# Seven PSUM banks in the first layer's loop, its sums and a residue on GpSimd, half the maxima rows on ScalarE

## What is computed

```python
def _L0_conv_ref(x, w_proj, b_proj, w_out, b_out):
    tokens = x.reshape(B, C, N).transpose(0, 2, 1)
    qkv = (tokens @ w_proj + b_proj).reshape(B, N, NUM_HEADS, 3 * HEAD_DIM)
    q, k, v = jnp.split(qkv, 3, axis=-1)
    attn = jnp.einsum('bihd,bjhd->bijh', q, k) * SCALE
    attn = jax.nn.softmax(attn, axis=2)
    res = jnp.einsum('bijh,bjhd->bihd', attn, v).reshape(B, N, NUM_HEADS * HEAD_DIM)
    out = res @ w_out + b_out + tokens
    return out.transpose(0, 2, 1).reshape(B, C, H, W)
```

## Time and profile before

| | us |
|---|---|
| median of three runs | 3099.82 (3094.11 to 3104.37) |
| the profiled execution | 3101.73, span 3100.0 |
| TensorE busy in it | 2708.6 (87%), mean granted clock 0.935 |
| VectorE busy | 2196.4 (71%) |
| ScalarE busy | 1220.1 (39%) |
| GpSimd busy | 603.8 (19%) |

### The profile page before, as it was taken

One profiled execution on the slowest core, in us unless ns is written; L12 is line 12 of the kernel. 1 busy time (PEld: TensorE's weight loads), 2 busy tenths in 40 slices (PEclk: granted clock), 3 DMA queues, 4 the chain that ended last, 5 costly groups with the idle time before them and its releaser, 6 DMA issues.

```text
span 3100.0 us, 42243 instructions
## 1 busy us (share of the span) xinstructions
PE 2708.6 (87%) x14966; PEld 1854.5 (60%) x14966; DVE 2196.4 (71%) x2490; ACT 1220.1 (39%) x1348; POOL 603.8 (19%) x381
## 2 busy tenths in 40 slices
PE   5989979899898898988889888898888899888993
PEld 4447754577545775467754677447764477644772
DVE  4876678766687676867678576785678766787666
ACT  2443325433254333543335333353334533245334
POOL 0520116002160022500224002330024200242011
PEclk8999989999799998999989999899999999899996
DMA  6100050000500005000040001400022000310016
GB/s 154 27 25 1 1 130 1 25 1 14 117 1 25 1 14 117 1 25 1 21 110 1 25 1 38 93 7 19 1 69 62 25 1 1 94 37 25 1 55 244
DMA packets 46388, 124.57 MB, mean 40 GB/s; under 512 B 9792, under 2 KB 21312, under 8 KB 42560
## 3 DMA queue, kind: packets, MB, share of 16 engines
q1 hardware_dynamic: 46144, 121.41, 14.4%
HBM read 43.01 MB, written 23.86 MB: 22 GB/s over the span
## 4 chain that ended last, share of the span: by engine, by line
PE 69%; DVE 10%; ACT 8%; issue 6%; SPq 4%; DMA 3%; DVEq 0%; ACTq 0%
PE tile L1270 23%; PE pv L1270 10%; PE pv L1374 7%; PE tile L1364 6%; PE tile L1342 5%; ACT p L666 4%; PE tile L1515 4%; SPq L452 3%; PE tile L1394 3%; DMA stack<-qk_r 2%; DVE small L877 2%; PE tile L1537 2%; PE tile L1645 2%; PE tile L1564 1%; PE tile L1416 1%
## 5 line engine op out<-in xcount | busy, mean ns | idle before, releaser
L877 DVE TENSOR_REDUCE small<-tile 128x1 f32<-128x1024 f32 x512 | 612.6, 1220 | 125.0 <-PE tile L1342 121.1
L666 ACT ACTIVATE p<-tile 128x1024 f32<-128x1024 f32 x512 | 506.7, 1026 | 457.9 <-PE tile L1364 393.4
L1342 PE MATMUL tile<-stack 96*128 96x512 f32 x1024 | 356.9, 441 | 63.6 <-DMA stack<-qk_r 30.3
L1364 PE MATMUL tile<-stack 112*128 112x512 f32 x1024 | 369.0, 452 | 20.8 <-DVE small L877 14.1
L1270 PE MATMUL tile<-qk_r 128*128 128x512 f32 x1536 | 377.9, 395 | 0.0
L578 POOL TENSOR_TENSOR row_sum<-act 128x256 f32<-128x256 f32 x32 | 42.1, 1335 | 1640.0 <-DVE act L1105 1640.0
L553 POOL TENSOR_TENSOR acc<-acc,p 128x1024 f32<-128x1024 f32 x144 | 344.8, 2416 | 31.2 <-DVE acc L909 29.3
L1270 PEld LDWEIGHTS tile<-qk_r 128*128 128x128 f32 x1536 | 287.1, 188 | 66.4 <-issue 7.7
L1110 DVE TENSOR_TENSOR pl<-p,ph 128x1024 fp32r<-128x1024 f32 x128 | 158.2, 1236 | 238.0 <-ACT p L751 238.0
L1364 PEld LDWEIGHTS tile<-stack 112*128 112x128 f32 x1024 | 175.2, 196 | 241.7 <-issue 85.0
L1342 PEld LDWEIGHTS tile<-stack 96*128 96x128 f32 x1024 | 185.9, 202 | 187.2 <-ACT p L666 110.8
(11 more groups left out here) (277 smaller groups left out, 4256.0 us busy)
## 6 DMA issues: line engine op xcount, KB each, us to landing
stack<-qk_r SPq DMA_DIRECT2D x192, 256.0 KB, 5.0
x_in<-in_x_dram SPq DMA_DIRECT2D x9, 1024.0 KB, 7.6
act<-in_x_dram SPq DMA_DIRECT2D x8, 1024.0 KB, 8.0
x_scratch<-act SPq DMA_DIRECT2D x7, 1024.0 KB, 4.0
z_scratch<-zbuf SPq DMA_DIRECT2D x7, 1024.0 KB, 5.1
stack<-ones SPq DMA_DIRECT2D x8, 512.0 KB, 7.6
w3f<-w3f_scratch SPq DMA_DIRECT2D x8, 512.0 KB, 3.2
fin_rest<-z_scratch SPq DMA_DIRECT2D x3, 1024.0 KB, 12.7
```

What stands on the lines that cost most here:

```text
L666: sc.activation(p0[:, jt % DEPTH, pair, :], tile_wait(b, "st0", *u, jt, pair), ACT.Exp, scale=float(D) ** -0.5).then_inc(scalar_done, scal ...
L877: ve.tensor_reduce(maxima[:, h * NT + it:h * NT + it + 1], t[:], X, ALU.max).then_inc(vector_done, vector.one("max0", g, h, it))
L1342: ins = mm(o[:, s], stack[0:IMAX, 0, g, h, it * P:(it + 1) * P], stack[0:IMAX, 1, g, h, s], start=True, stop=True)
L1364: ins = mm(o[:, halves[k]], stack[0:K0, 1, g, h, jt * P:(jt + 1) * P], stack[0:K0, 0, g, h, halves[half]], start=True, stop=True)
```

## The change

1. In units 0 to 2 the six banks and the idle bank of `pv` are handed out in two rings. `s0`, `m0`, `den0` and (in units 1 and 2) `ex0` share two tiles of two banks. The scores have three single banks, one of them the idle half of `pv`, and one head to a bank: four `st0` and four `exp0` of 128x512 a step in place of two of 128x1024. The order in a step becomes `s0`, `st0`, `st0`, `s0`, `st0`, `st0`, `pv0`. Unit 3 keeps two heads to a tile and the three large tiles.
2. All ten `add0` of units 0 to 2 go to GpSimd.
3. `res_lo` of units 0 to 2 goes to GpSimd, behind the two additions of step 1 of the next unit. The bias `bv0` is no longer added in `res_hi` and `res_lo`: it is multiplied by the output weights once, in the setup, and comes in with the output bias.
4. Of the four `max_rows` of a unit VectorE keeps two. For the other two heads ScalarE runs four `max_cols`, each an activation of 16x2x128 out of `m0`'s tile with `mask8` as its scale, before the first `exp0` of the unit.

```diff
-POOL_BOTH = (1, 2, 4)
+POOL_BOTH = (1, 2, 3, 4, 5)
+    if next_unit(g, half):
+        return ("s0", 0), ("st0", 0), ("st0", 1), ("s0", 1), ("st0", 2), ("st0", 3)
+    return ("st0", 0), ("st0", 1)
...
+        s += [("pv0_out", *last_unit(*u))] if last_unit(*u) else []
+        s += [("max_cols", *u, t) for t in range(HT)]
...
-            s += [("res_lo", *last)] if last and jt == 3 else []
-            s += [("max_rows", *following, h) for h in range(G)]
+            s += [("max_rows", *following, h) for h in range(G // 2)]
...
+            s += [("add0", *u, jt, pair) for pair in range(2) if adder(*u, jt, pair) == "pool"]
+            s += [("res_lo", *last_unit(*u))] if last_unit(*u) and jt == 1 else []
...
+        ring = ("scores" if kind == "st0" else "rows") if looped else "whole"
+        if ring == "scores":
+            home[n] = ((2, 0), (2, 1), (3, 1 - n[2]))[rings[ring] % 3]
+        else:
+            home[n] = (rings[ring] % (2 if ring == "rows" else SLOTS), None)
...
+                            pool.wait_ge(scalar_done, scalar.at(b, "res_hi", g, half))
+                            pe.tensor_tensor(side[:, 1, g, cols_], raw[:, cols_], side[:, 0, g, cols_].bitcast(F32),
+                                             ALU.subtract).then_inc(pool_done, gps.one("res_lo", g, half))
...
+                    for t in range(HT):
+                        it = HT * half + t
+                        sc.activation(stack[IMAX:K0, 0, g, G // 2:G, it * P:(it + 1) * P], m, ID, scale=mask8[:, it:it + 1]
+                                      ).then_inc(scalar_done, scalar.one("max_cols", g, half, t))
```

More of the change, by code:

```diff
@@ L68, in last_unit, with score_tiles, heads_of, exp_of @@
     return UNITS[k - 1] if k else None
+def score_tiles(g, half):
+    return 2 if (g, half) == UNITS[-1] else G
+def heads_of(g, half, k):
+    n = G // score_tiles(g, half)
+    return range(n * k, n * k + n)
+def exp_of(g, half, jt, pair):
+    return ("exp0", g, half, jt, score_tiles(g, half) // 2 * (pair + 1) - 1)
+def key_tile(g, half):
+    if next_unit(g, half):
+        return ("s0", 0), ("st0", 0), ("st0", 1), ("s0", 1), ("st0", 2), ("st0", 3)
+    return ("st0", 0), ("st0", 1)
 def rows_of(unit, k):
@@ L244, in conv_seq_kernel, with banks, leavers @@
     place = {n: k for k, n in enumerate(tiles)}
-    def slot(*name):
[L247 to L255, removed]
+    home, rings = {}, {"whole": 0, "rows": 0, "scores": 0}
+    for n in tiles:
+        kind, unit, looped = n[0], n[1:3], False
+        if kind in ("st0", "den0"):
+            looped = unit != UNITS[-1]
+        elif kind == "s0":
+            looped = n[3] // HT + n[1] > 0
+        elif kind == "m0":
+            looped = unit != UNITS[0]
+        elif kind == "ex0":
+            looped = next_unit(*unit) not in (None, UNITS[-1])
+        ring = ("scores" if kind == "st0" else "rows") if looped else "whole"
[3 more added lines that the diff above has]
+            home[n] = (rings[ring] % (2 if ring == "rows" else SLOTS), None)
+        rings[ring] += 1
+    def slot(*name):
+        assert home[name][1] is None
+        return home[name][0]
+    def banks(name):
+        k, half = home[name]
+        return [(k, q) for q in range(2) if half in (None, q)]
+    def leavers(b, *name):
+        k, found = place[name], {}
+        for bank in banks(name):
+            users = [n for n in tiles[k + 1:] + tiles[:k] if bank in banks(n)]
+            if bank[0] == SLOTS:
+                users = [n for n in tiles[:k] if bank in banks(n) and n[1:3] == name[1:3]]
+            for engine, *step in last_readers(users[-1]) if users else ():
+                steps = {"scalar": scalar, "vector": vector}[engine]
+                now = place[users[-1]] < k
+                found[engine] = max(found.get(engine, (False, 0, None)), (now, steps.place[tuple(step)], tuple(step)))
+        return [(engine, ({"scalar": scalar, "vector": vector}[engine].at if now
+                          else {"scalar": scalar, "vector": vector}[engine].before)(b, *step))
+                for engine, (now, _, step) in found.items()]
     x_v = x.rearrange("b (t p) h w -> b p t (h w)", p=P)
@@ L595, in tile_wait @@
                 act_e.wait_ge(tensor_done, tensor.at(b, *name))
[L596 removed]
+                return where(*name)
             act_e.wait_ge(weights_in[0], 16)
@@ L686, in _ @@
                     last = last_unit(*u)
+                    if last:
+                        pv0_out(*last)
+                    max_cols(*u)
                     for jt in range(NT):
[L688 to L691, removed]
+                        for k in range(score_tiles(*u)):
+                            exp0(u, jt, k)
                         if last and jt == 2:
@@ L991, in _ @@
                                 add0(u, jt - 1, pair)
-                        if last and jt == 3:
-                            res_lo(*last)
                     if following:
```

120 lines of the change are left out of this document (74 added, 46 removed).

## The result

| | before | after |
|---|---|---|
| median us | 3102.1 (3094.11 to 3104.51, 4 runs) | 3209.07 (3203.78 to 3213.39, 4 runs) |
| the profiled execution | 3101.73, span 3100.0 | 3213.39, span 3211.7 |
| mean granted clock in it | 0.935 | 0.917 |

The account below looks back on a forecast made before the run. It took the tile ring to pace the old step and GpSimd's additions to hold `den0` after the change. Losses of 2.6 + 0.95 + 0.95 + 1.1 us a pass, 45 in all, plus 36 for the clock: median 3181; range 3115 to 3230.

Parts of the forecast that it names:

- GpSimd as the bound of units 1 and 2: Units 1 and 2: `den0` waits for GpSimd's additions and starts at 31.3 us instead of 30.35, plus 0.95 each.
- The step: Clean step of units 0 to 2: 3.2 us in place of 3.50 with three single banks for the scores.
- Unit 0: Start of unit 0: four `max_cols` delay the first `s0`, and `den0` starts at 491.3 instead of 488.67, plus 2.6 us.
- Unit 3: Start of unit 3: first scores fall into `den0`'s tile and wait for `rec0`, plus 1.1 us.
- The negation: End of a unit: three small VectorE operations negating the maxima; by the port rule up to two additions late.
- Rival 3: Negation blocked as well: 0.6 us more in each of 24 units and longer standstills, 3225 us; chance 8%.
- The clock: TensorE's clock falls to 0.50 around `den0` after standstills: 1.5 us for each of 24 stretches, 36 us.
- The sum at full clock: All units, clock held: 5.6 us a pass, 45 for eight passes, giving 3147 us on the profiled execution.
- VectorE gives up two `max_rows`: nothing: VectorE in each unit: two `max_rows` fewer, 1.24 us, gain nothing because `den0` covers them.
- Rival 2: TensorE sets the end: units 1 and 2 gain 2.4 us each, 3070 us in all; chance 6%.
- Rival 4: No change: `res_hi` earlier, `res_lo` and `max_cols` at low bounds, clock held, about 3108 us; chance 6%.
- rival 1: TensorE's clock holds through the waits before `den0`, all else as forecast, 3145 us; chance 25%.

Follow-up runs that it names:

- the five-step kernel: Changed kernel with GpSimd summing steps 1 to 4, `den0` taking step 5, all `max_rows` on VectorE, unit 3's first scores skipping `den0`'s tile: 3037.74 us, ratio 0.9798.
- The ring alone: Changed kernel with eight sums on GpSimd, `res_lo` on VectorE and no `max_cols`, keeping part 1 and the bias move: 3120.0 us, ratio 1.0071.
- the run with additions that need each other: Changed kernel with `res_lo` back on VectorE in step 3 and GpSimd adding pairs in order 0, 1, 1, 0, 0, 1: 3167.43 us, ratio 1.0223.
- the run with the order alone: Changed kernel, otherwise whole, with GpSimd's ten sums in pair order 0, 1, 1, 0, 0, 1: 3205.87 us, ratio 1.0359.

## Why the prediction held, and where it was short

The direction and the mechanism were right, and the time fell inside the range, 28 us above the forecast. By its own steps:

- **GpSimd as the bound of units 1 and 2: right.** Forecast were its start 5.2 into the unit, a pause of 1.0 before `res_lo`, and its end at 31.2. The rows have 5.2, 0.98 and 30.8. The residue took 1.28, near the 1.2 taken.
- **The step: nearly right.** 3.2 forecast, 3.08 measured; TensorE was through with `pv0` at 26.8, so the standstill before `m0` was 4.42, not 3.4.
- **Unit 0: right in kind, 2.6 forecast, 3.1 measured.** Four `max_cols` took 1.53 (1.9 taken). The run without the columns confirms that they are the cause. There `den0` comes 3.7 earlier than with them, so they cost more than the 3.1 that the change shows, and the rest of the change gains 0.6 in unit 0.
- **Unit 3: right.** 1.1 forecast, 1.0 in six passes, with the idle time before the first scores put down to `rec0`, as forecast. In two passes it was 2.2 and 2.5; these are the two in which the low clock lasted longest in unit 2's `den0` (5.3).
- **The negation: a case that was held for a rival.** The forecast put `den0` 0.1 behind GpSimd's last addition, with `m0` done before. Rival 3 said that the negation would be blocked and `m0` follow it. So it came (5.04 for `neg_hi`), and `den0` starts 1.40 after the last addition (543.23 to 544.63), of which 0.95 is `m0` at the low clock. This is why units 1 and 2 lost 1.84 and 1.74 and not 0.95 although GpSimd was 0.4 early. The rival had 8%, with the text's own reason for it, that the operations meet an addition every time. The chance was too low: nothing in the rows of before spoke for the negation getting in. The rival's reason, turns of one instruction each, is not what came either: `neg_hi` alone waited past two boundaries between additions.
- **The clock: the term that was mis-sized.** 36 us were taken, 1.5 for each `den0`, as the middle between 0 and 2.8. The run with TensorE kept busy measures 62 in all, 2.6 for each. In units 1 and 2 the low stretch covers most of `den0` (4.56 to 5.31 in place of 2.83, so 1.7 to 2.5 over); in unit 0 five of eight had none and three had 1.3 to 2.2. The `den0` stretches together are 39, near the 36, but `m0` and the stretches outside the loop had no term in the sum.
- **The sum at full clock: close by luck.** With the clock held the kernel has 3147 us, and the sum was 3145 on the median. The units of that run are 6.7 a pass longer than before, 53 in all, where 45 was forecast. Its time agrees because it is 8 shorter outside the loop, for which the forecast had no term.
- **"VectorE gives up two `max_rows`: nothing": right.** With them back, units 1 and 2 kept their 32.2. **The setup, under 1 us: not shown.** 2.4 us were lost before the first `m0`, where the setup lies, and no run splits them. The same stretch differs by up to 3.2 between runs with one and the same setup.

Rival 2, in which TensorE sets the end, is what the five-step kernel shows: with GpSimd done in time, all `max_rows` on VectorE and the tile skipped, the same ring gives 2.0%. The ring alone lost as well (25 us), since VectorE's operations then waited for GpSimd and unit 3's first scores for `rec0`. So most of the loss is in what went with the ring: GpSimd's longer queue, the standstills with the low clock behind them, and the columns in unit 0. Rival 4 did not come, and rival 1, the clock holding, came only in five of unit 0's eight waits.

## What to carry to other kernels

Give an engine with a small busy share its work by the deadline in the stage where it works: here GpSimd was at 19%, and ten additions in a unit made it the last to finish, where eight did not. Summing five steps, with all `max_rows` on VectorE and unit 3's tile skipped, turned 3.5% slower into 2.0% faster. When an edit makes a busy engine wait, count the low clock behind that wait near the upper bound and add what runs beside it: 2.6 us for each wait here, where 1.5 was taken. When VectorE works on SBUF beside GpSimd, look for the longest run of independent instructions on GpSimd, since that run, not one instruction, is what VectorE may have to wait for.

## What was not expected of the hardware

**VectorE can wait for several of GpSimd's instructions, not for one.** Beside GpSimd's additions of 2.38 us, an operation of VectorE whose tensors all lie in SBUF took up to 11.1 us (`res_lo`, 0.68 alone), 3.4 (128x1024 additions, 1.2 alone) and 5.07 (a 128x16 operation with one tensor as input, 0.17 alone). In each of these it ended 0.03 to 1.1 us after the end of an addition behind which GpSimd paused, if only for the 0.08 us in which the next addition waits for that one's result. The form of the instruction made no difference (11.12 and 11.14 at the most); making each step's first addition depend on the one before cut the longest from 11.1 to 2.38 and 90 us from the kernel. The one case in which VectorE got in between two independent additions was during the first addition behind a pause, and then always (24 times in the run with additions that need each other, 24 in the run with the order alone). What in the chip does this is not shown. VectorE's maxima, which read PSUM, kept 1.22 us (1219 ns in the mean) all the while, and so did `res`, with one operand in SBUF and one in PSUM: 0.69 beside an addition (L1019).

**Work that nothing needs can pay.** Twelve matmuls of no use, 3.0 us a unit, gave 62 us: the wait before `m0` fell from 4.42 to 1.51 and the clock stayed at 1.00. In the run with the additions' order alone the wait was in two pieces, 2.23 and 1.28, with 1.0 us of `m0` between, and the clock fell to 0.50 there as well.
